# Encoder of a token tower: the products with the values one slot later, two dense units side by side, and the second norm between two pairs of row maxima

## The chip, the cores and the metric

One core of a Trainium2 chip runs the whole program. Its engines are TensorE (PE: matmuls; PEld: loading of their weights), VectorE (DVE), ScalarE (ACT), GpSimd (POOL) and SyncE (SP, which here only issues DMAs). The metric is the device time of one execution in microseconds; a kernel's time is the median of its runs.

## The reference

Eight sequences of 256 tokens, 256 features, float32 throughout. Four encoder layers come first. Then follow a second attention (16 heads of 64, windows of 128) and a mixture of 16 experts with two shared ones. The change touches the encoder alone:

```python
for l in range(4):
    y = layer_norm(h)                        # first norm
    q, k, v = y @ wq + bq, y @ wk + bk, y @ wv + bv      # 16 heads of 16
    p = softmax(q @ k.T / 4)                 # 256 x 256 a head
    h = h + (p @ v) @ wo + bo
    y = layer_norm(h)                        # second norm
    h = h + relu(y @ w1 + b1) @ w2 + b2      # 256 -> 1024 -> 256
```

## The kernel before, in words

**Jobs and slots.** The encoder is a pipeline of 32 jobs, one for each layer and sequence, `j` from 0 to 31. `for j in range(JOBS + 2)` with `for c in range(GROUPS)` inside gives every job four slots. In slot `(j, c)` TensorE computes the scores of four heads' pairs (`scores`, L401; four row strips of 32, so four matmuls go side by side into PSUM banks 0 to 3). VectorE takes their row maxima (`row_max`, L716), ScalarE takes the exponentials (`exps`, L547, two instructions for each of the four banks). In the next slot TensorE transposes the probabilities in four calls (`turn_probs` 0 to 3, L414) into banks 4 and 5 by turns. VectorE copies transpositions 0 and 2 out to `pts` (L724), ScalarE 1 and 3 (L556). So transposition 2 can start once copy 0 has freed bank 4, and transposition 3 once copy 1 has freed bank 5. Then come the products with the values (`pv`, L430; four column strips of 32, bank 6).

**Dense units.** Between these stand the wide matmuls of neighbouring jobs: in slot 0 the values of job j (L375) and half of the second feed-forward product of job j-2 (`ffn_down`, L458); in slot 1 the output projection of job j-1 (L375) and the other half; in slot 2 queries and keys of job j+1 (L367) and the first quarter of the first feed-forward product of job j-1 (`ffn_up`, L446); in slot 3 its other three quarters. A short transposition (L341) stands in each of slots 0 to 2: that of the softmax sums (`r_T`), of the first norm (`y_T`) and of the second norm (`y2_T`).

**What sets the order.** Each engine has one in-order instruction stream, which the code writes out by hand. The engines meet at semaphores, one pair for each PSUM bank (filled, freed). The list `order` says which bank each unit uses; a unit waits until the bank's last user has been taken out. VectorE also does the norms: `stats_of` writes mean and variance, GpSimd takes the root (L306), and `normalise` (L675, L677, L680) writes the normed rows. `attended` (L754) adds the output projection to `h`, `bias` (L747) the bias, `fed_forward` (L763) the second feed-forward product.

In this text a TensorE group is one call: eight matmul records for a dense unit (sixteen for half of `ffn_down`), eight for two transpositions of probabilities, four for a short one, sixteen for scores, thirty-two for products with the values.

Of the kernel before, what the change touches and what calls it, by code (L numbers as in the profile page):

```python
# [135 lines left out]
def embed_and_encoder(nc, io, h, ident, weights, wqkv, wout, norm, normab, gamma, pmk, w_yT, w_qT0, w_kT0):  # L136

    JOBS = L * B
    GROUPS = 4
    ctx = ExitStack()  # L140
    with ctx:
# [49 lines left out]
        def use(u, b):  # L191
            if 0 <= u[0] < JOBS:
                order.append((u, b))

        use((0, "yT"), 4), use((0, "q"), 7), use((0, "k"), 5)
        for j in range(JOBS + 2):
            for c in range(GROUPS):
                for n in range(4):
                    use((j, "S", 4 * c + n), n)
                if c == 0:  # L200
                    use((j, "v"), 7), use((j - 1, "rT"), 0), use((j - 2, "down", 0), 7)
                if c == 1:
                    use((j - 1, "wo"), 7), use((j + 1, "yT"), 0), use((j - 2, "down", 1), 7)
# [4 lines left out]
                jp, cp = divmod(GROUPS * j + c - 1, GROUPS)  # L208
                for n in range(4):
                    use((jp, "pt", 4 * cp + n), 4 + n % 2)  # L210
                if cp == 0:
                    use((jp, "o"), 6)
# [120 lines left out]
        def _(pe):  # L333
# [45 lines left out]
            def values(j):  # L379
                if j == 0:  # L380
                    pe.wait_ge(s_rest, 32)
                if real(j):
                    token_major(j, "v", yT[0], 2)

            def project_out(j):
                if real(j):
                    evacuated(pe, (j, "o"))
                    token_major(j, "wo", oT, 3)

            def scores(j, c):  # L390
                if not real(j):
                    return
                if c == 0:
                    evacuated(pe, (j, "q"))
                    evacuated(pe, (j, "k"))
                qt, ch = c // 2, c % 2
                gs = [acquire(pe, (j, "S", 4 * c + n)) for n in range(4)]
                for odd in range(2):
                    for n in range(4):
                        r = slice(32 * n, 32 * n + 32)  # L400
                        last = pe.matmul(gs[n][:, odd * S:(odd + 1) * S], qm[j % 2][r, odd, ch, qt * P:(qt + 1) * P],  # L401
                                         kT[j % 2][r, ch, :], start=True, stop=True)
                        if odd:
                            filled(last, (j, "S", 4 * c + n))
# [78 lines left out]
            feature_major(0, "k", 1)  # L483
            for j in range(JOBS + 2):
                for c in range(GROUPS):
                    jp, cp = divmod(GROUPS * j + c - 1, GROUPS)
                    scores(j, c)
                    if c == 0:
                        values(j)
                    if c == 1:  # L490
                        project_out(j - 1)
                    if c == 2:
                        feature_major(j + 1, "q", 0)
                    if c == 3:
                        ffn_up(j - 1, 1)
                    turn_probs(jp, cp, 0)
                    turn_probs(jp, cp, 1)
                    if c == 0:
                        r_T(j - 1)
                    if c == 1:  # L500
                        y_T(j + 1)
                    if c == 2:
                        y2_T(j - 1)
                    if c == 3:
                        ffn_up(j - 1, 2)
                    turn_probs(jp, cp, 2)
                    turn_probs(jp, cp, 3)
                    if (j, c) == (JOBS + 1, 0):
                        for u in SECOND[j, c]:
                            second(u)  # L510
                    if c < 2:
                        ffn_down(j - 2, c)
                    if c == 2:
                        feature_major(j + 1, "k", 1)
                    if c == 3:
                        ffn_up(j - 1, 3)
                    pv(jp, cp)
                    if (j, c) != (JOBS + 1, 0):
                        for u in SECOND.get((j, c), ()):
                            second(u)  # L520
                    if c == 2:
                        ffn_up(j - 1, 0)

        @block.scalar
        def _(act):
# [76 lines left out]
            for j in range(JOBS + 2):  # L602
                for c in range(GROUPS):
                    jp, cp = divmod(GROUPS * j + c - 1, GROUPS)
                    exps(j, c, 0)
                    exps(j, c, 1)
                    copy_pt(jp, cp, 1)
                    exps(j, c, 2)
                    if c == 0:
                        r_out(j - 1)  # L610
                    if c == 1:
                        y_out(j + 1, "yT", 0)
                    if c == 2:
# [5 lines left out]
                    if c != 2:  # L619
                        copy_pt(jp, cp, 3)  # L620
                    if c == 2:
                        k_out(j + 1)
                    for u in SECOND.get((j, c), ()):
                        second_out(u)
                    if c == 2:
                        relu(j - 1, 0)

        @block.vector
        def _(dve):
# [120 lines left out]
            def attended(j):  # L750
                if not real(j):
                    return
                g = take(dve, (j, "wo"))
                release(nc.vector.tensor_tensor(h[:, j % B], h[:, j % B], g[:].rearrange("p (i d) -> p i d", i=NT), ALU.add), (j, "wo"))  # L754
                evacuated(dve, (j, "wo"))
                bias(j, R_BO)

            def fed_forward(j, i):
                if not real(j):
# [33 lines left out]
            for j in range(JOBS + 2):  # L793
                for c in range(GROUPS):
                    jp, cp = divmod(GROUPS * j + c - 1, GROUPS)
                    if c == 0:
                        recips(j - 1)
                    if c == 1:
                        fed_forward(j - 2, 0)
                        o_norm(j - 1)  # L800
                    if c == 2:
                        fed_forward(j - 2, 1)
                    row_max(j, c, 0)
                    row_max(j, c, 1)
                    row_max(j, c, 2)
                    row_max(j, c, 3)
                    copy_pt(jp, cp, 0)
                    if c == 0:
                        v_out(j)
                        if j > 0:  # L810
                            stats_of(1, j + 1)
                    if c == 1:
# [6 lines left out]
                    copy_pt(jp, cp, 2)  # L819
                    if c == 0:  # L820
                        normalise(1, j + 1)
                    if c == 1:
                        normalise(2, j - 1)
                    if c == 2:
                        bias(j - 1, R_B2)
                    if c == 3:
                        relu(j - 1, 3)
                    if 0 <= GROUPS * (j - JOBS + 4) + c < 5:
                        second_norm(0, GROUPS * (j - JOBS + 4) + c)
                    if 0 <= GROUPS * (j - JOBS + 3) + c - 1 < 4:  # L830
                        second_norm(1, GROUPS * (j - JOBS + 3) + c - 1)
                    if (j, c) == (JOBS - 1, 0):
                        for w in range(NT):
                            nc.vector.tensor_copy(w_kT0[:, :, w, 0:PM], pmk[:, :, 0, :])
                    if (j, c) == (JOBS + 1, 0):
                        second_k_out(0)
                    if (j, c) == (JOBS + 1, 2):
                        for i in (1, 2, 3):
                            second_k_out(i)
# [1254 lines left out]
```

## Time and profile before

| | |
|---|---|
| median of 3 runs | 2105.56 us (2102.9 to 2107.07) |
| profiled execution | 2102.53 us, span 2100.7 us |
| TensorE clock granted, mean | 0.993 of full speed |
| busy over the span | PE 97%, PEld 79%, DVE 62%, ACT 49%, POOL 10% |
| encoder | first scores at 22.6 us, end of the stage at 1314 us |
| second attention, shared experts, experts | 1314 to 2101 us |

Matmuls are pipelined, so that a PE row is also busy while a matmul drains. What a group really costs is the time from its first start to the next group's first start, and that is how the rows below are to be read.

### The profile page before, as it was taken

What the parts mean: (1) busy time and instruction counts of PE and PEld (TensorE: products, weight loads), DVE (VectorE), ACT (ScalarE), POOL (GpSimd) and SP (SyncE); (2) the same over time, 40 slices, a digit from 0 to 9 for tenths busy, and PEclk for the clock granted to TensorE, in tenths of its full rate; (3) what the DMA queues carried; (4) which work ended last, traced back from release to release, by engine and by line L of the source; (5) the groups of instructions that cost most, each with busy time, mean ns of one, the idle gap of its engine ahead of it and who ended that gap; (6) DMA issues with size and microseconds to landing.
All of it is one profiled execution on the core that took longest, in us unless ns stands there. A gap on an engine that the chain in (4) does not pass through costs nothing. (4 is left out here: it accounts for less than half of the span.)

```text
span 2100.7 us, 42201 instructions
## 1 busy us (share of the span) xinstructions
PE 2037.0 (97%) x16462; PEld 1657.2 (79%) x16462; DVE 1299.0 (62%) x3344; ACT 1031.9 (49%) x3525; POOL 215.8 (10%) x251
## 2 busy tenths in 40 slices
PE   5899999999999999999999999899999999999998
PEld 4688888888888888888888877678788788877776
DVE  4676767676676776766767863767777646423322
ACT  3666656656566565666656552545445531111111
POOL 4000000000000000000000000000000000234444
PEclk9999999999999999999999999999999999999999
DMA  6000000100000400000000000500000100025542
GB/s 182 1 1 2 1 2 2 69 1 2 1 2 1 155 2 2 2 2 1 2 2 2 2 1 1 183 1 1 1 1 1 61 1 11 24 78 165 156 142 65
DMA packets 27203, 69.84 MB, mean 33 GB/s; under 512 B 9920, under 2 KB 17825, under 8 KB 23680
## 3 DMA queue, kind: packets, MB, share of 16 engines
q1 hardware_dynamic: 18432, 59.42, 8.4%
q0 software_dynamic: 6400, 5.63, 1.1%
q8 instruction: 134, 2.20, 0.4%
q10 hardware_dynamic: 2176, 2.10, 0.3%
q14 instruction: 61, 0.50, 0.1%
HBM read 61.16 MB, written 17.40 MB: 37 GB/s over the span
## 5 line engine op out<-in xcount | busy, mean ns | idle before, releaser
L547 ACT ACTIVATE probs<-bank,nmax 128x256 f32<-128x256 f32 x1024 | 474.4, 478 | 413.1 <-DVE nmax L716 413.1
L716 DVE TENSOR_REDUCE nmax<-bank 128x2 f32<-128x512 f32 x512 | 317.9, 683 | 208.6 <-PE bank L401 205.4
L414 PE MATMUL bank<-ident,probs 128*128 128x128 f32 x2048 | 271.9, 276 | 5.1 <-DVE pts L724 5.1
L414 PEld LDWEIGHTS bank<-ident,probs 128*128 128x128 f32 x2048 | 232.6, 141 | 39.7 <-DVE pts L724 22.5
L446 PE MATMUL bank<-yT,weights 128*128 128x256 f32 x1024 | 248.3, 386 | 0.9 <-ACT aT L570 0.9
L458 PE MATMUL bank<-weights,aT 128*128 128x256 f32 x1024 | 232.6, 380 | 1.3 <-DVE h L754 0.8
L547 ACT ACTIVATION_READ_ACCUMULATOR probs<-bank,nmax 128x1 f32 x1024 | 216.0, 211 | 0.0
L446 PEld LDWEIGHTS bank<-yT,weights 128*128 128x128 f32 x1024 | 184.5, 190 | 37.7 <-ACT aT L570 11.6
L458 PEld LDWEIGHTS bank<-weights,aT 128*128 128x128 f32 x1024 | 189.5, 190 | 25.3 <-DVE h L754 1.2
L724 DVE COPY pts<-bank 128x512 f32<-128x512 f32 x256 | 172.8, 675 | 38.6 <-PE bank L414 38.5
L556 ACT ACTIVATE pts<-bank 128x512 f32<-128x512 f32 x256 | 156.8, 612 | 21.4 <-PE bank L414 18.7
L306 POOL TENSOR_TENSOR sd<-mv,half 128x2 f32<-128x2 f32 x64 | 44.2, 690 | 1168.6 <-DVE mv L668 1168.6
L401 PE MATMUL bank<-kT,qm 32*128 32x256 f32 x2048 | 150.4, 408 | 3.7 <-ACT probs L547 2.8
L430 PE MATMUL bank<-pts,v 128*32 128x128 f32 x4096 | 140.9, 279 | 8.8 <-ACT pts L556 8.8
L430 PEld LDWEIGHTS bank<-pts,v 128*32 128x32 f32 x4096 | 105.9, 111 | 50.8 <-issue 38.9
L1334 ACT ACTIVATE w_probs<-w_bank,w_nmax 128x144 f32<-128x144 f32 x256 | 108.2, 536 | 75.6 <-DVE w_nmax L1499 75.6
L1890 PE MATMUL e_bank<-xeT,wqkv 128*128 128x320 f32 x512 | 140.8, 433 | 0.8 <-DVE xeT L1960 0.8
L367 PE MATMUL bank<-yT,weights 128*128 128x256 f32 x512 | 126.9, 392 | 1.2 <-ACT yT L534 1.2
L1890 PEld LDWEIGHTS e_bank<-xeT,wqkv 128*128 128x128 f32 x512 | 95.9, 190 | 39.0 <-issue 1.2
L1213 PE MATMUL w_bank<-xT_all,weights 128*128 128x256 f32 x512 | 121.1, 389 | 4.1 <-DVE weights L1594 2.9
L401 PEld LDWEIGHTS bank<-kT,qm 32*128 32x128 f32 x2048 | 94.6, 188 | 37.6 <-issue 28.4
L367 PEld LDWEIGHTS bank<-yT,weights 128*128 128x128 f32 x512 | 94.1, 194 | 23.2 <-issue 10.9
(218 smaller groups left out, 2935.4 us busy)
## 6 DMA issues: line engine op xcount, KB each, us to landing
wqkv<-in_experts SPq DMA_DIRECT2D x16, 1024.0 KB
weights<-in_wtok SPq DMA_DIRECT2D x4, 2048.0 KB, 19.0
wqkv<-in_experts SPq DMA_DIRECT2D x16, 512.0 KB
expert_rows<-xT_all SPq DMA_DIRECT2D x10, 546.0 KB, 16.5
xrows<-expert_rows SPq DMA_DIRECT2D x16, 273.0 KB
weights<-in_wtok SPq DMA_DIRECT2D x3, 1024.0 KB
wqkv<-in_wqkv SPq DMA_DIRECT2D x1, 3072.0 KB, 17.5
weights<-in_shared SPq DMA_DIRECT2D x1, 3072.0 KB, 10.8
```

What stands on the lines that cost most here:

```text
L367: last = pe.matmul(g[:, m * S:(m + 1) * S], wqkvo[buf(j)][:, n, k, m * P:(m + 1) * P], yT[0][:, k, :], start=(k == 0), stop=(k == KD - 1))
L401: last = pe.matmul(gs[n][:, odd * S:(odd + 1) * S], qm[j % 2][r, odd, ch, qt * P:(qt + 1) * P], kT[j % 2][r, ch, :], start=True, stop=True)
L414: last = pe.transpose(g[:, (NT * x + kb) * P:(NT * x + kb + 1) * P], p[:, x, kb * P:(kb + 1) * P], ident[:])
L430: last = pe.matmul(out, v[j % 2][:, kb, 4 * ch + n, x, :], pts[(4 * c + n) % 8][:, x, kb, :], start=(x == 0 and kb == 0), stop=(x == 1 and ...
L446: last = pe.matmul(g[:, m * S:(m + 1) * S], w1[buf(j)][:, k, f * P:(f + 1) * P], yT[1][:, k, :], start=(k == 0), stop=(k == KD - 1))
L458: last = pe.matmul(g[:, 0:D], aT[:, f, i * P:(i + 1) * P], w2[buf(j)][:, f, :], start=(f == 0), stop=(f == FT - 1))
L547: last = nc.scalar.activation(probs[u % 8][:, x, :], g[:, x * S:(x + 1) * S], ACT.Exp, bias=nmax[j % 2][:, col:col + 1], accum_out=rsum[j ...
L556: release(nc.scalar.activation(pts[(4 * c + n) % 8][:], g[:].rearrange("p (x k s) -> p x k s", x=2, k=NT), ACT.Copy), u)
L716: nc.vector.tensor_reduce(nmax[j % 2][:, col:col + 2], g[:].rearrange("p (x s) -> p x s", x=2), AX.X, ALU.max, negate=True).then_inc(s_max, 1)
L724: release(nc.vector.tensor_copy(pts[(4 * c + n) % 8][:], g[:].rearrange("p (x k s) -> p x k s", x=2, k=NT)), u)
L1213: last = pe.matmul(g[:, x * S:(x + 1) * S], w[e][:, k, m * P:(m + 1) * P], xT[:, k, (2 * t + a) * S:(2 * t + a + 1) * S], start=(k == 0), ...
L1890: last = pe.matmul(g[:, 0:CAP], (w1, w3)[x][a][:, k, m * P:(m + 1) * P], xeT[a][:, k, :], start=(k == 0), stop=(k == KD - 1))
```

## The change

The instructions and their sizes stay; the order on TensorE, ScalarE and VectorE and the use of the banks change.

- `pv` takes the group of two slots before, not of one, and stands right behind `scores`.
- Transpositions 0 and 1 follow it; then two dense units side by side (in slot 2 with `y2_T` between them); then transpositions 2 and 3, and at the slot's end `r_T`, `y_T` or the fourth unit.
- In slot 1 the second feed-forward product now precedes the output projection.
- The banks: in slot 0 `ffn_down` goes to bank 0 and `r_T` to 7, in slot 1 the projection to bank 1 and `y_T` to 7.
- ScalarE does all four `exps` of a slot in a row, then copy 1; the copies of `r_T` and `y_T` and the first `relu` move to the head of the following slot.
- VectorE: the second norm is written in slot 2 between row maxima 1 and 2; its statistics follow copy 2 of slot 1; `fed_forward` moves into the slot of its product; the bias of the projection is added a slot ahead of the projection.

```diff
@@ tensor
                     scores(j, c)
+                    pv(jq, cq)
+                    turn_probs(jp, cp, 0)
+                    turn_probs(jp, cp, 1)
                     if c == 0:
                         values(j)
+                        ffn_down(j - 2, 0)
                     if c == 1:
+                        ffn_down(j - 2, 1)
                         project_out(j - 1)
                     if c == 2:
                         feature_major(j + 1, "q", 0)
+                        y2_T(j - 1)
+                        feature_major(j + 1, "k", 1)
                     if c == 3:
                         ffn_up(j - 1, 1)
-                    turn_probs(jp, cp, 0)
-                    turn_probs(jp, cp, 1)
+                        ffn_up(j - 1, 2)
+                    turn_probs(jp, cp, 2)
+                    turn_probs(jp, cp, 3)
...
-                    pv(jp, cp)
...
@@ scalar
-                    exps(j, c, 0)
-                    exps(j, c, 1)
-                    copy_pt(jp, cp, 1)
-                    exps(j, c, 2)
...
+                    if c == 3:
+                        relu(j - 1, 0)
+                    for n in range(4):
+                        exps(j, c, n)
                     if c == 2:
                         y_out(j - 1, "y2T", 1)
-                        copy_pt(jp, cp, 3)
-                    exps(j, c, 3)
+                    copy_pt(jp, cp, 1)
+                    if c == 2:
+                        k_out(j + 1)
                     if c == 3:
                         relu(j - 1, 2)
...
+                    copy_pt(jp, cp, 3)
@@ vector
+                    row_max(j, c, 0)
+                    row_max(j, c, 1)
                     if c == 1:
-                        fed_forward(j - 2, 0)
                         o_norm(j - 1)
                     if c == 2:
-                        fed_forward(j - 2, 1)
+                        normalise(2, j - 1)
                     row_max(j, c, 2)
                     row_max(j, c, 3)
...
                     if c == 1:
+                        fed_forward(j - 2, 1)
                         attended(j - 1)
-                        stats_of(2, j - 1)
...
                     copy_pt(jp, cp, 2)
+                    if c == 1:
+                        stats_of(2, j - 1)
                     if c == 0:
                         normalise(1, j + 1)
-                    if c == 1:
-                        normalise(2, j - 1)
+                        bias(j - 1, R_BO)
```

How it stands on TensorE in slot 0 of a job in the steady pipeline, before. L401 are the scores, L375 the values, L414 transpositions of probabilities, L341 the short transposition, L458 half of the second feed-forward product, L430 the products with the values:

```order
L401 MATMUL bank<-kT,qm 128x256 x8
L375 MATMUL bank<-weights,yT 128x256 x4
L414 MATMUL bank<-ident,probs 128x128 x8
L341 MATMUL bank<-ident,rb 128x128 x4
L414 MATMUL bank<-ident,probs 128x128 x8
L458 MATMUL bank<-weights,aT 128x256 x8
L430 MATMUL bank<-pts,v 32x128 x16
```

And of the changed kernel, whose lines are numbered one higher here:

```order
L402 MATMUL bank<-kT,qm 128x256 x8
L431 MATMUL bank<-pts,v 32x128 x16
L415 MATMUL bank<-ident,probs 128x128 x8
L376 MATMUL bank<-weights,yT 128x256 x4
L459 MATMUL bank<-weights,aT 128x256 x8
L415 MATMUL bank<-ident,probs 128x128 x8
L342 MATMUL bank<-ident,rb 128x128 x4
```

The two column- and row-strip groups now stand side by side, and 12 dense matmuls stand between the two pairs of transpositions where 4 short ones stood.

TensorE in slot 2, before (L367 queries and keys, L446 the first quarter of the feed-forward product):

```order
L401 MATMUL bank<-kT,qm 128x256 x8
L367 MATMUL bank<-yT,weights 128x256 x4
L414 MATMUL bank<-ident,probs 128x128 x8
L341 MATMUL bank<-ident,yn 128x128 x4
L414 MATMUL bank<-ident,probs 128x128 x8
L367 MATMUL bank<-yT,weights 128x256 x4
L430 MATMUL bank<-pts,v 32x128 x16
L446 MATMUL bank<-yT,weights 128x256 x4
```

After:

```order
L402 MATMUL bank<-kT,qm 128x256 x8
L431 MATMUL bank<-pts,v 32x128 x16
L415 MATMUL bank<-ident,probs 128x128 x8
L368 MATMUL bank<-yT,weights 128x256 x4
L342 MATMUL bank<-ident,yn 128x128 x4
L368 MATMUL bank<-yT,weights 128x256 x4
L415 MATMUL bank<-ident,probs 128x128 x8
L447 MATMUL bank<-yT,weights 128x256 x4
```

The products no longer stand between two dense units.

VectorE from the projection of slot 1 to the end of the maxima of slot 2, before (L754 `attended`, L747 bias, L664 and L668 statistics, L724 copy 2, L675 to L680 the second norm, L763 `fed_forward`, L716 row maxima):

```order
L754 TENSOR_TENSOR h<-h,bank 128x512
L747 TENSOR_TENSOR h<-h,rows 128x512
L651 MEMSET scratch 128x1
L664 BN_STATS stats<-h 128x6 x2
L651 MEMSET scratch 128x1
L668 BN_AGGR mv<-stats 128x2 x2
L724 COPY pts<-bank 128x512
L675 TENSOR_SCALAR den<-sd 128x2
L677 RECIPROCAL rstd<-den 128x2
L680 TENSOR_SCALAR yn<-h,mv,rstd 128x256 x2
L763 TENSOR_TENSOR h<-h,bank 128x256
L716 TENSOR_REDUCE nmax<-bank 128x2 x4
```

After (the same work at L751, L720, L660, L664, L671 to L676, L712):

```order
L751 TENSOR_TENSOR h<-h,bank 128x512
L720 COPY pts<-bank 128x512
L647 MEMSET scratch 128x1
L660 BN_STATS stats<-h 128x6 x2
L647 MEMSET scratch 128x1
L664 BN_AGGR mv<-stats 128x2 x2
L712 TENSOR_REDUCE nmax<-bank 128x2 x2
L671 TENSOR_SCALAR den<-sd 128x2
L673 RECIPROCAL rstd<-den 128x2
L676 TENSOR_SCALAR yn<-h,mv,rstd 128x256 x2
L712 TENSOR_REDUCE nmax<-bank 128x2 x2
```

The second norm has moved out of slot 1 and stands between the second and the third row maximum of slot 2.

## Rows read from the trace of the kernel before

**Rows 1.** Busy time by stretch (start:end, length, engines, clock), slots of the filling pipeline.
```profile
41.18:50.64 9.46, 9.11 (x85) 7.06 (x81) 5.58 (x10) 5.72 (x20) 0.54 (x1) 0.85 0.00 1
50.64:58.93 8.29, 4.82 (x69) 3.66 (x65) 4.55 (x8) 4.73 (x18) 0.00 (x0) 0.93 0.01 2
58.93:68.91 9.98, 7.85 (x80) 6.05 (x77) 6.50 (x20) 5.32 (x19) 0.72 (x1) 0.84 0.00 0
68.91:79.72 10.81, 8.25 (x79) 6.45 (x76) 7.78 (x19) 5.75 (x20) 0.68 (x1) 0.82 0.01 2
79.72:90.64 10.92, 10.92 (x96) 8.55 (x93) 6.08 (x11) 6.47 (x22) 0.00 (x0) 0.91 0.01 2
90.64:99.85 9.21, 9.21 (x89) 7.66 (x88) 5.46 (x11) 6.40 (x22) 0.00 (x0) 1.00 0.01 2
```

**Rows 2.** Timeline of TensorE, slot 3: start, duration, line, out<-in, records.
```profile
405.39 1.89 PE L446 MATMUL bank<-yT,weights 128*128 128x256 f32 x8
407.12 1.04 PE L414 MATMUL bank<-ident,probs 128*128 128x128 f32 x8
```

**Rows 3.** Timeline of TensorE, slot 0.
```profile
410.82 1.15 PE L401 MATMUL bank<-kT,qm 32*128 32x256 f32 x16
411.90 1.99 PE L375 MATMUL bank<-weights,yT 128*128 128x256 f32 x8
413.73 1.04 PE L414 MATMUL bank<-ident,probs 128*128 128x128 f32 x8
414.61 0.60 PE L341 MATMUL bank<-ident,rb 128*128 128x128 f32 x4
415.12 1.09 PE L414 MATMUL bank<-ident,probs 128*128 128x128 f32 x8
416.05 3.64 PE L458 MATMUL bank<-weights,aT 128*128 128x256 f32 x16
419.63 1.08 PE L430 MATMUL bank<-pts,v 128*32 128x128 f32 x32
420.64 0.71 PE L401 MATMUL bank<-kT,qm 32*128 32x256 f32 x8
```

**Rows 4.** Timeline of TensorE, slot 2, its head and its end.
```profile
430.43 1.15 PE L401 MATMUL bank<-kT,qm 32*128 32x256 f32 x16
...
437.55 1.08 PE L430 MATMUL bank<-pts,v 128*32 128x128 f32 x32
...
440.48 1.15 PE L401 MATMUL bank<-kT,qm 32*128 32x256 f32 x16
```

**Rows 5.** Timeline of VectorE, slots 1 and 2.
```profile
421.80 2.48 DVE L716 TENSOR_REDUCE nmax<-bank 128x2 f32<-128x512 f32 x4 [0.23 <-PE bank L401]
424.20 0.68 DVE L724 COPY pts<-bank 128x512 f32<-128x512 f32 x1
...
426.24 0.42 DVE L664 BATCH_NORM_STATS2 stats<-h 128x6 f32<-128x256 f32 x1
...
428.08 0.17 DVE L675 TENSOR_SCALAR den<-sd 128x2 f32<-128x2 f32 x1 [0.23 <-POOL sd L306]
...
428.48 0.74 DVE L680 TENSOR_SCALAR yn<-h,mv,rstd 128x256 f32<-128x256 f32 x2
```

**Rows 6.** Timeline of ScalarE, slot 2.
```profile
432.38 0.47 ACT L547 ACTIVATE probs<-bank,nmax 128x256 f32<-128x256 f32 x1 [3.95 <-DVE nmax L716]
...
435.35 0.48 ACT L547 ACTIVATE probs<-bank,nmax 128x256 f32<-128x256 f32 x1
...
435.80 1.03 ACT L534 ACTIVATE yT<-bank,cols 128x256 f32<-128x256 f32 x2
436.70 0.62 ACT L556 ACTIVATE pts<-bank 128x512 f32<-128x512 f32 x1
```

**Rows 7.** Timeline of ScalarE and TensorE in the filling pipeline.
```profile
56.58 0.65 ACT L556 ACTIVATE pts<-bank 128x512 f32<-128x512 f32 x1
...
57.37 1.63 PE L430 MATMUL bank<-pts,v 128*32 128x128 f32 x32 [1.37 <-ACT pts L556]
```

More of the change, by code:

```diff
@@ L199, in embed_and_encoder @@
                     use((j, "S", 4 * c + n), n)
+                jp, cp = divmod(GROUPS * j + c - 1, GROUPS)
+                jq, cq = divmod(GROUPS * j + c - 2, GROUPS)
+                if cq == 0:
+                    use((jq, "o"), 6)
+                for n in range(4):
+                    use((jp, "pt", 4 * cp + n), 4 + n % 2)
                 if c == 0:
-                    use((j, "v"), 7), use((j - 1, "rT"), 0), use((j - 2, "down", 0), 7)
+                    use((j, "v"), 7), use((j - 2, "down", 0), 0), use((j - 1, "rT"), 7)
                 if c == 1:
-                    use((j - 1, "wo"), 7), use((j + 1, "yT"), 0), use((j - 2, "down", 1), 7)
+                    use((j - 2, "down", 1), 7), use((j - 1, "wo"), 1), use((j + 1, "yT"), 7)
                 if c == 2:
@@ L207, in embed_and_encoder @@
                     use((j - 1, "up", 1), 7), use((j - 1, "up", 2), 0), use((j - 1, "up", 3), 7)
[L208 to L212, printed above, removed]
                 for n, u in enumerate(SECOND.get((j, c), ())):
@@ L486, in _ @@
                     jp, cp = divmod(GROUPS * j + c - 1, GROUPS)
+                    jq, cq = divmod(GROUPS * j + c - 2, GROUPS)
                     scores(j, c)
+                    pv(jq, cq)
+                    turn_probs(jp, cp, 0)
+                    turn_probs(jp, cp, 1)
+                    if (j, c) == (JOBS + 1, 0):
+                        for u in SECOND[j, c]:
+                            second(u)
                     if c == 0:
                         values(j)
+                        ffn_down(j - 2, 0)
                     if c == 1:
+                        ffn_down(j - 2, 1)
                         project_out(j - 1)
@@ L501, in _ @@
                         y_T(j + 1)
[L502 to L516, printed above, removed]
-                    pv(jp, cp)
                     if (j, c) != (JOBS + 1, 0):
@@ L522, in _ @@
                         ffn_up(j - 1, 0)
+                    if c == 3:
+                        ffn_up(j - 1, 3)
         @block.scalar
@@ L604, in _ @@
                     jp, cp = divmod(GROUPS * j + c - 1, GROUPS)
-                    exps(j, c, 0)
-                    exps(j, c, 1)
-                    copy_pt(jp, cp, 1)
-                    exps(j, c, 2)
-                    if c == 0:
+                    if c == 1:
                         r_out(j - 1)
-                    if c == 1:
+                    if c == 2:
                         y_out(j + 1, "yT", 0)
+                    if c == 3:
+                        relu(j - 1, 0)
+                    for n in range(4):
+                        exps(j, c, n)
                     if c == 2:
                         y_out(j - 1, "y2T", 1)
-                        copy_pt(jp, cp, 3)
-                    exps(j, c, 3)
+                    copy_pt(jp, cp, 1)
+                    if c == 2:
+                        k_out(j + 1)
                     if c == 3:
                         relu(j - 1, 2)
[L619 to L622, printed above, removed]
+                    copy_pt(jp, cp, 3)
                     for u in SECOND.get((j, c), ()):
                         second_out(u)
-                    if c == 2:
-                        relu(j - 1, 0)
         @block.vector
@@ L752, in attended @@
                     return
+                step.wait(dve)
                 g = take(dve, (j, "wo"))
@@ L755, in attended @@
                 evacuated(dve, (j, "wo"))
-                bias(j, R_BO)
             def fed_forward(j, i):
@@ L811, in _ @@
                             stats_of(1, j + 1)
+                        fed_forward(j - 2, 0)
                     if c == 1:
+                        fed_forward(j - 2, 1)
                         attended(j - 1)
[L814 removed]
                     if c == 2:
@@ L819, in _ @@
                     copy_pt(jp, cp, 2)
+                    if c == 1:
+                        stats_of(2, j - 1)
                     if c == 0:
                         normalise(1, j + 1)
-                    if c == 1:
-                        normalise(2, j - 1)
+                        bias(j - 1, R_BO)
                     if c == 2:
+                        if real(j - 1):
+                            dve.wait_ge(s_yn[1], j)
                         bias(j - 1, R_B2)
```

2 lines of the change are left out of this document (removed).

## The prediction, written before the changed kernel ran

> **What bounds the kernel now.** I read the summary of the busy times first, then the busy time by stretch, then the timeline of TensorE alone over one job, and last the timelines of VectorE and ScalarE beside it. The summary puts TensorE at 97% of the span. In a slot of the steady pipeline it is busy for the whole of it, 9.21 of 9.21 us, at the full clock of 2.4 GHz, with VectorE at 5.46 and ScalarE at 6.40 [rows 1]. So TensorE sets the encoder's pace, and the question is what its slots hold besides work. The Trainium skill says of that (Trainium Kernel Development and Optimization, Performance Expectations) that matmul busy time is a bad measure since matmuls are pipelined; this trace agrees, the row of 9.21 busy us hides all that follows.
>
> Distances from start to start show it. I call the matmuls of 128 rows and columns full, the scores (32 rows) and the products with the values (32 columns) strips.
> - A full dense unit of eight records takes 1.73 between full ones (405.39 to 407.12) [rows 2], and 1.83 behind scores (411.90 to 413.73) [rows 3]. Between products and scores it takes 1.92 (2.93 from 437.55 to 440.48, less 1.01 for the products) [rows 4]; less the 0.10 that it pays behind strips that is 1.82 before scores alone.
> - Two transpositions take 0.88 (413.73 to 414.61), and 0.93 where their first had to wait or follows strips (415.12 to 416.05) [rows 3]. So one takes 0.44.
> - Scores take 1.08 to what follows (410.82 to 411.90); products 1.01 before scores (419.63 to 420.64) [rows 3].
> - The short transposition takes 0.51 (414.61 to 415.12), 0.44 for its four records and 0.07 of waiting for VectorE's copy 0, which frees bank 4 [rows 3].
>
> Every change between strips and full, or between the two strips, thus costs about 0.2, half at the end of the one, half at the head of the other; waits for data are small. The lengths are: slot 0 9.82 (410.82 to 420.64), slot 1 9.79 (to 430.43) [rows 3, 4], slot 2 10.05 (430.43 to 440.48) [rows 4], slot 3 9.21 [rows 1]. A job takes 38.87.
>
> **The change part by part.**
>
> *Order on TensorE.* I add the new order up from the same distances.
> - Slot 0: scores 1.08, products 1.01, transpositions behind strips 0.93, values 1.73, second feed-forward product 2 x 1.73 = 3.46, transpositions 0.88, short one with the change to scores 0.44 + 0.09 = 0.53: 9.62. That is 0.20 less.
> - Slot 1 has the same parts: 9.62, 0.17 less.
> - Slot 2: 1.08 + 1.01 + 0.93 + 1.73 + 0.44 + 1.73 + 0.88 + 1.82 = 9.62, 0.43 less. One pair of changes is gone here, as the products no longer stand between two dense units.
> - Slot 3: 1.08 + 1.01 + 0.93 + 3.46 + 0.88 + 1.82 = 9.18, 0.03 less.
>
> Without new waits a job takes 38.04, which is 0.83 less.
>
> *Products right behind scores.* The trace has no such pair. Products took 1.01 behind full units, and scores 1.08 before them [rows 3]. Low end: these two less the 0.1 that either change costs at its border, should two strip groups overlap. High end: products pay at their head what a dense unit pays behind scores, 0.10 [rows 3, 2]. I take 1.08 and 1.01, because each is the group's own row, and keep 0.10 a slot, 0.4 a job, for the range.
>
> *Waits that go.* Transposition 2 now stands behind 5.2 us of dense work in slots 0 and 1 and behind 3.9 in slot 2, so copy 0 is long done. The products wait for copies 2 and 3 of the slot before; ScalarE's copy 3 ends 0.3 to 0.4 after the scores start, and VectorE's copy 2 in slot 1 ends about 0.2 after it, and the products start at 1.08. That cover is 0.7.
>
> *Waits that come: slot 2.* Times from the scores' first start.
> 1. VectorE. In slot 1 the projection is now the last dense unit; its last record ends at 1.08 + 1.01 + 0.93 + 3.46 + 1.73 and some 0.15 of drain = 8.36. Then come the addition and copy 2 (0.68 for a copy as wide [rows 5], and the same for the addition) and the statistics (about 1.05 of the 1.84 from 426.24 to 428.08; the rest is GpSimd's root) [rows 5]. VectorE is free at 10.85, which is 1.24 of slot 2.
> 2. Row maxima take 0.62 each (2.48 for four) [rows 5]: 0 and 1 end at 2.48. The root was ready at 2.0. The second norm takes 1.14 (428.08 to 429.22) [rows 5]: 3.64.
> 3. Exponentials start 0.72 behind their maximum (1.95 from the scores' start to the first, of which 1.23 to the first maximum) [rows 4, 6] and follow each other at 0.45 (435.35 to 435.80) [rows 6]. Those of banks 2 and 3 run from 4.37 to 6.18.
> 4. ScalarE then writes out the second norm's transposition, 0.90 to its next start (435.80 to 436.70), and only then copy 1, 0.62 [rows 6]: 7.70. TensorE starts 0.14 behind the end of such a copy (57.23 to 57.37) [rows 7]: 7.84.
> 5. TensorE has queued transposition 3 behind 1.08 + 1.01 + 0.93 + 1.73 + 0.44 + 1.73 + 0.44 = 7.36. It waits 0.48 and restarts at 0.05: 0.53. Behind it wait the first feed-forward quarter and the next scores.
>
> So slot 2 takes 10.15, 0.1 more than before. The bounds are 0 (if ScalarE gets to copy 1 half a us sooner) and 1.0 (if the norm's root comes late by as much as its 0.5 of slack). In slots 0, 1 and 3 copy 1 ends at about 6.9, 6.9 and 6.3, and transposition 3 stands at 8.6, 8.6 and 6.9; the least cover is 0.6.
>
> *Banks.* Bank 0 for the feed-forward product in slot 0 is asked for at 4.75, and its exponentials are out at 3.4. Its addition on VectorE ends at 8.8, and the next scores want the bank at 9.6. Bank 7 for that quarter in slot 2 needs the queries' copy, which ends at 7.5, before 7.8. I cost them at nothing; the last is the thinnest.
>
> *VectorE.* Its work of a job is unchanged. In slot 0 the first norm and the bias now reach 1.8 us into slot 1, which puts that slot's exponentials 0.6 later, covered as above.
>
> Steady sum: -0.83 + 0.53 = -0.30 a job, over the 30 jobs in which the pipeline is full: -9.
>
> **The filling of the pipeline.** Five slots from 41.18 to 90.64 take 9.46, 8.29, 9.98, 10.81 and 10.92 with the clock at 0.82 to 0.93 [rows 1]: TensorE waits for the last copies before the products (1.37 in one place [rows 7]), and after such waits runs part of the way at 1.2 GHz. Products a slot later take that wait away. What is late next is the chain scores, exponentials, copy 1, transposition 3: 1.95 + 8 x 0.45 + 0.62 + 0.14 + 0.44 = 6.8, with the short transposition 7.3. By that the five slots are 7.4 (sum of TensorE's parts), 6.8, 7.3, 8.6 (1.3 for a VectorE that starts late by its norm and bias) and 10.15: 40.2 for 49.5, or -9. Some time at 1.2 GHz will stay, as waits of 1.4 us remain. I take -8, bounds -4 and -10.5. The drain of the pipeline has the same units in another order; I leave it at nothing, within 1.5.
>
> **Sum.** -9 - 8 = -17 on the profiled 2102.5 (span 2100.7 and 1.8 around it) gives 2085.5. The median of the runs shown is 3.0 above the profiled execution, so 2088.6 there; I say 2088.
>
> **The rivals.**
> - *The wait of slot 2 doesn't come* (or is under 0.15), because ScalarE is ahead of my chain. For it: ScalarE is busy 6.4 of 9.2 [rows 1]. Against it: the chain is in order and each link has a row. Then 30 x 0.83 = 25 and 8: 2105.6 - 33 = 2073. Chance 0.16.
> - *Other waits take the gain*: copies or bank 7 late in a slot where I see 0.3 to 0.7 of cover; the job gives back its 0.3, and only some of the filling stays. 2098 to 2109. For it: VectorE runs later than before in three slots of four. Against it: no cover is under 0.3. Chance 0.12.
> - *Scores and products side by side cost more than apart*, which ends slower. Place: the four new pairs in each job. If the products can't start until the last scores have left the array and their own weights are then loaded, each pair pays up to 0.3 more, 30 x 4 x 0.3 = 36, so 2088 + 36 = 2124; the change is slower from 17 / 120 = 0.14 a pair. Against it: products followed by scores, the same pair turned round, cost 1.01 and no more [rows 3]. Chance 0.08. The Trainium skill (TensorEngine Tiling (Array Packing), Key Properties) says that a change of tiling mode drains TensorE. It gives no price; by it the four pairs each pay a whole change, and so they do in my sum, at the rows' 0.2; the trace agrees for the turned pair, and no run so far shows this one.
> - That the change doesn't do what it says is excluded by the order shown ahead.
>
> **How the numbers follow.** The forecast has 0.64 and its own range is 2077 to 2097. The rivals have 0.16 below, 0.12 around no change and 0.08 above. The range reaches down to 2072 and up to 2101. About 0.2%, some 4 us, is what a measurement of this kernel can tell from no change. Faster by more: 0.64 + 0.16 + 0.04 = 0.84; within it 0.07; slower 0.09.
>
> **What would show it.** In the timeline of TensorE after: scores to products 1.08, products to transpositions 1.01, transpositions 0.93; slots 0 and 1 at 9.6, slot 3 at 9.2 and a wait of about 0.5 at transposition 3 of slot 2, put down to ScalarE's copy. Before 91 us, slots of 7 to 9 us and a clock above 0.9. I am wrong if slots 0, 1 or 3 show a wait over 0.1, if scores to products takes over 1.2, or if slot 2 is under 9.8.

## The result and the profile after

The changed kernel takes 2074.07 us (median of 4 runs, 2070.51 to 2075.57) against 2105.61 for the kernel before: ratio 0.9851, 95% interval [0.9836, 0.9867]. The profiled execution has a span of 2072.9 us against 2100.7. The forecast was 2088, with a range of its own of 2077 to 2097; the measured time lies 3 us below that range.

The sum was -17, the measured change of the span is -27.8 (the medians differ by 31.5, the change timed once more below by 27.2). Cut at the first starts of the score groups in both traces, it falls apart as follows (us):

| stretch | before | after | difference |
|---|---|---|---|
| start to the first scores | 22.56 | 22.07 | -0.5 |
| filling, jobs 0 and 1 | 77.30 | 69.11 | -8.2 |
| jobs 2 to 27 | 1010.67 | 993.38 | -17.3 |
| jobs 28 to 30 | 118.18 | 116.97 | -1.2 |
| job 31 to the end of the encoder | 84.97 | 86.15 | +1.2 |
| second stage to its first transposition | 12.97 | 11.06 | -1.9 |
| the rest | 774.1 | 774.2 | +0.1 |

Two rows of this table can't be put to the change. In the second stage's row the granted clock was 0.87 in the trace before and 1.00 in the one after. Over all twelve traces of this document that stretch takes 11.0 to 11.6 us where the clock is 1.00, and 12.4 to 14.5 where it is lower, whatever the order. The rest takes 774.0 to 774.3 in five of the twelve and 776.0 to 776.1 in seven; that this pair agrees to 0.1 says little.

TensorE alone, slot 0 of a job in the steady pipeline (start, duration, group), to be read against [rows 3]:

```profile
396.83 1.15 PE L402 MATMUL bank<-kT,qm 32*128 32x256 f32 x16
397.91 1.08 PE L431 MATMUL bank<-pts,v 128*32 128x128 f32 x32
398.92 1.09 PE L415 MATMUL bank<-ident,probs 128*128 128x128 f32 x8
399.85 1.89 PE L376 MATMUL bank<-weights,yT 128*128 128x256 f32 x8
401.58 3.62 PE L459 MATMUL bank<-weights,aT 128*128 128x256 f32 x16
405.03 1.04 PE L415 MATMUL bank<-ident,probs 128*128 128x128 f32 x8
405.91 0.60 PE L342 MATMUL bank<-ident,rb 128*128 128x128 f32 x4
406.44 0.93 PE L402 MATMUL bank<-kT,qm 32*128 32x256 f32 x12
```

From start to start the distances are 1.08, 1.01, 0.93, 1.73, 3.45, 0.88 and 0.53: the slot is 9.61 long, with no wait in it. Scores followed by products, the pair that the trace of before did not show, cost what they cost apart.

Slot 2, the same view, against [rows 4]:

```profile
416.04 1.15 PE L402 MATMUL bank<-kT,qm 32*128 32x256 f32 x16
...
422.95 1.26 PE L415 MATMUL bank<-ident,probs 128*128 128x128 f32 x8
424.05 1.89 PE L447 MATMUL bank<-yT,weights 128*128 128x256 f32 x8
425.87 0.70 PE L402 MATMUL bank<-kT,qm 32*128 32x256 f32 x6
```

Transpositions 2 and 3 take 1.10 and not 0.88: here is the new wait, 0.22 with its restart, and the slot is 9.83 long. VectorE and ScalarE show what it hangs on; VectorE first:

```profile
417.16 0.15 DVE L664 BATCH_NORM_AGGREGATE mv<-stats 128x2 f32<-128x6 f32 x1
417.23 1.26 DVE L712 TENSOR_REDUCE nmax<-bank 128x2 f32<-128x512 f32 x2
418.41 0.16 DVE L671 TENSOR_SCALAR den<-sd 128x2 f32<-128x2 f32 x1
...
418.80 0.74 DVE L676 TENSOR_SCALAR yn<-h,mv,rstd 128x256 f32<-128x256 f32 x2
...
419.46 1.28 DVE L712 TENSOR_REDUCE nmax<-bank 128x2 f32<-128x512 f32 x2
```

ScalarE in the same slot:

```profile
420.17 0.47 ACT L547 ACTIVATE probs<-bank,nmax 128x256 f32<-128x256 f32 x1 [0.31 <-DVE nmax L712]
...
421.99 1.03 ACT L534 ACTIVATE yT<-bank,cols 128x256 f32<-128x256 f32 x2
422.88 0.62 ACT L556 ACTIVATE pts<-bank 128x512 f32<-128x512 f32 x1
```

The chain is the forecast one: the statistics keep VectorE until the maxima start at 1.19 of the slot, the norm stands between the two pairs, and ScalarE writes out `yT` before copy 1, which ends at 7.46. The links on VectorE are shorter than I took them, and so is the step from copy 1 to TensorE; those on ScalarE have the forecast lengths.

Slots of the filling pipeline, busy time by stretch, against [rows 1]. They are slot 3 of job 0 and slots 0 to 2 of job 1; the last figures of a row are the granted clock, the share of the DMA engines and GB/s:

```profile
46.85:53.59 6.74, 4.42 (x64) 3.25 (x65) 4.73 (x9) 4.77 (x18) 0.00 (x0) 1.00 0.00 0
53.59:61.68 8.09, 8.04 (x77) 6.12 (x76) 4.62 (x12) 5.22 (x19) 0.00 (x0) 0.79 0.01 2
61.68:72.18 10.50, 8.07 (x77) 6.32 (x76) 7.21 (x18) 5.28 (x20) 0.72 (x1) 0.84 0.01 2
72.18:82.01 9.83, 9.83 (x93) 8.04 (x93) 8.28 (x22) 7.77 (x25) 0.69 (x1) 1.00 0.01 2
```

The first three are 6.74, 8.09 and 10.50 for 8.29, 9.98 and 10.81. In the middle two the clock is at 1.2 GHz for part of the way (0.79 and 0.84 of full speed): behind a wait of 2.43 us the projection takes 3.44 (67.29 to 70.73) where it takes 1.73 at full clock. In a second profile of the same kernel these two slots took 7.21 and 8.12.

### The profile page after: what moved, and what is told of

It is laid out like the page before. It is cut to its first block and busy times, and to the rows that moved or that the text cites. A ratio compares the mean times of both kernels' runs of the same rounds, so it can differ in the third digit from the quotient of the medians.

```text
span 2072.9 us, 42265 instructions
## 1 busy us (share of the span) xinstructions
PE 2013.2 (97%) x16462; PEld 1659.8 (80%) x16462; DVE 1299.1 (63%) x3344; ACT 1039.5 (50%) x3525; POOL 215.8 (10%) x251
## 5 line engine op out<-in xcount | busy, mean ns | idle before, releaser
L547 ACT ACTIVATE probs<-bank,nmax 128x256 f32<-128x256 f32 x1024 | 469.4, 481 | 230.3 <-DVE nmax L712 230.3
L712 DVE TENSOR_REDUCE nmax<-bank 128x2 f32<-128x512 f32 x512 | 322.1, 681 | 78.0 <-PE bank L402 78.0
L415 PE MATMUL bank<-ident,probs 128*128 128x128 f32 x2048 | 281.6, 278 | 12.6 <-DVE pts L720 6.9
L447 PE MATMUL bank<-yT,weights 128*128 128x256 f32 x1024 | 237.9, 381 | 0.9 <-ACT aT L570 0.9
L720 DVE COPY pts<-bank 128x512 f32<-128x512 f32 x256 | 175.6, 686 | 59.0 <-PE bank L415 55.3
L447 PEld LDWEIGHTS bank<-yT,weights 128*128 128x128 f32 x1024 | 188.1, 191 | 23.2 <-ACT aT L570 1.3
L368 PE MATMUL bank<-yT,weights 128*128 128x256 f32 x512 | 123.0, 385 | 1.2 <-ACT yT L534 1.2
L1212 PEld LDWEIGHTS w_bank<-xT_all,weights 128*128 128x128 f32 x512 | 95.3, 192 | 17.9 <-DVE weights L1593 3.6
```

What stands on the lines that cost most here:

```text
L368: last = pe.matmul(g[:, m * S:(m + 1) * S], wqkvo[buf(j)][:, n, k, m * P:(m + 1) * P], yT[0][:, k, :], start=(k == 0), stop=(k == KD - 1))
L415: last = pe.transpose(g[:, (NT * x + kb) * P:(NT * x + kb + 1) * P], p[:, x, kb * P:(kb + 1) * P], ident[:])
L447: last = pe.matmul(g[:, m * S:(m + 1) * S], w1[buf(j)][:, k, f * P:(f + 1) * P], yT[1][:, k, :], start=(k == 0), stop=(k == KD - 1))
L547: last = nc.scalar.activation(probs[u % 8][:, x, :], g[:, x * S:(x + 1) * S], ACT.Exp, bias=nmax[j % 2][:, col:col + 1], accum_out=rsum[j ...
L712: nc.vector.tensor_reduce(nmax[j % 2][:, col:col + 2], g[:].rearrange("p (x s) -> p x s", x=2), AX.X, ALU.max, negate=True).then_inc(s_max, 1)
L720: release(nc.vector.tensor_copy(pts[(4 * c + n) % 8][:], g[:].rearrange("p (x k s) -> p x k s", x=2, k=NT)), u)
```

## Experiments

Eight edits in ten runs, one of them the changed kernel again and one a repetition. In what follows "a job" is one of the steady ones, from score group to score group: 38.87 before, 38.20 after (slots 9.60, 9.60, 9.83, 9.17).

### The changed kernel again

> The changed kernel itself, beside the three that build on it, so that they are compared on one chip: 2074 us, 0.985 of the kernel before. Its trace, like the first, should show slots of 9.60, 9.60, 9.83 and 9.17 us.

Measured: 2077.22 us, ratio 0.9871 [0.9856, 0.9886]; slots 9.60, 9.60, 9.83, 9.17. It is the base for the three that were timed beside it. Its filling takes 67.9 us, 1.2 less than in the first trace, and it has the low clock (0.86) at the second stage's start.

### The wait of slot 2 is the output that stands before copy 1

```diff
-                    if c == 2:
-                        y_out(j - 1, "y2T", 1)
                     copy_pt(jp, cp, 1)
                     if c == 2:
+                        y_out(j - 1, "y2T", 1)
                         k_out(j + 1)
```

> ScalarE takes copy 1 ahead of the output of the second norm's transposition in slot 2. Theory: the 0.22 us that transposition 3 waits in slot 2 is that output (0.90 from start to start) standing before copy 1; now copy 1 ends at 6.6 of the slot and transposition 3 stands at 7.4, so slot 2 falls from 9.83 to 9.61, 30 times 0.22 = 6.6 us, and up to 1 us more in slot 2 of the last job: 2067 us. Rival: the wait only moves to the first feed-forward quarter, which stands right behind and needs that output as well as the queries' copy: slot 2 stays within 0.1 of 9.83, 2074 us.

Measured: 2069.74 us, ratio 0.984 [0.9822, 0.9858], 7.5 under the changed kernel beside it; repeated, 2066.88 us, 0.983 [0.9809, 0.985]. Slot 2 of the timeline of TensorE:

```profile
413.40 1.15 PE L402 MATMUL bank<-kT,qm 32*128 32x256 f32 x16
...
420.31 1.04 PE L415 MATMUL bank<-ident,probs 128*128 128x128 f32 x8
421.18 1.89 PE L447 MATMUL bank<-yT,weights 128*128 128x256 f32 x8
423.01 0.50 PE L402 MATMUL bank<-kT,qm 32*128 32x256 f32 x4
```

The pair of transpositions is back at 0.87, the slot at 9.61, a job at 37.98. So the wait was that one link, and with it gone no wait is left in the steady job. Slot 2 of job 31 gains as well, 9.75 for 11.82 in the changed kernel beside it, where I had expected at most 1; the granted clock in that slot was 1.00 here and 0.86 there. The rival, that it moves on to the first feed-forward quarter, falls: that stands 0.87 behind the pair, without a wait. This version beats both kernels.

### The place of the second norm

Undone alone: `normalise(2, j - 1)` stands behind `stats_of(2, j - 1)` in slot 1 again.

```diff
-                    if c == 2:
-                        normalise(2, j - 1)
...
                     if c == 1:
                         stats_of(2, j - 1)
+                        normalise(2, j - 1)
```

> One part undone: the second norm stands at the end of slot 1 again, behind its statistics, all else as in the changed kernel. Theory: the place between two pairs of maxima is what keeps the dense order alive. Here VectorE waits for GpSimd's root until 1.95 of slot 2 and starts the row maxima at 3.05 and not 1.19; the exponentials end at 7.4, copy 1 at 8.9, and transposition 3, which stands at 7.4, waits 1.6: slot 2 takes 11.3, +1.5 a job, 30 x 1.5 = +44: 2118 us. Rival: its place is neutral because VectorE is busy 71% only: 2074 us.

Measured: 2123.59 us, ratio 1.011 [1.0086, 1.0133], slower than the kernel before. Slot 2 takes 11.36, a job 39.74. VectorE waits for the root where the maxima could run, and they start at 3.13 of the slot (430.71 is its start):

```profile
432.78 0.17 DVE L671 TENSOR_SCALAR den<-sd 128x2 f32<-128x2 f32 x1 [0.80 <-POOL sd L307]
...
433.84 2.48 DVE L712 TENSOR_REDUCE nmax<-bank 128x2 f32<-128x512 f32 x4
```

The other end of the chain, on TensorE:

```profile
438.37 0.60 PE L415 MATMUL bank<-ident,probs 128*128 128x128 f32 x4
439.76 0.66 PE L415 MATMUL bank<-ident,probs 128*128 128x128 f32 x4 [0.79 <-ACT pts L556]
```

Copy 1 on ScalarE, which it waits for:

```profile
439.06 0.65 ACT L556 ACTIVATE pts<-bank 128x512 f32<-128x512 f32 x1
```

A third thing came beside the forecast: a wait of 0.25 at the keys, for bank 1's exponentials. That the dense order pays at all hangs on the norm's new place, which is worth 1.53 a job here.

### Dense units side by side, but the products where they were

```diff
-                    pv(jq, cq)
                     turn_probs(jp, cp, 0)
...
                     if c == 3:
                         ffn_up(j - 1, 3)
+                    pv(jp, cp)
```

The list of banks follows the order.

> One part undone: products with the group of the slot before, at the slot's end behind transpositions 2 and 3 (and what follows them); the dense units stay side by side. Theory: the later products are needed for the rest. Here the products wait for ScalarE's copy 3 in slots 0 and 1 (0.5 each), and everything behind the scores comes 1 us sooner, so that transposition 3 waits for copy 1 by 1.1 in slot 2 and 0.4 in slot 3, and the change of form costs 0.05 more a slot: +2.5 a job: 2145 us. Rival: the gain is that of the dense units side by side alone, and the products' place is worth only its form changes: 2080 us.

Measured: 2153.88 us, ratio 1.0258 [1.0236, 1.028]. A job takes 40.53, +2.33 for a forecast of +2.5; the slots are 10.01, 10.17, 10.84 and 9.51. The profiled execution was the fastest of the four, 2146.20; the median is 9 above the forecast of 2145. Slot 0's products wait for ScalarE's copy 3, right behind the short transposition:

```profile
428.22 0.60 PE L342 MATMUL bank<-ident,rb 128*128 128x128 f32 x4
429.16 1.08 PE L431 MATMUL bank<-pts,v 128*32 128x128 f32 x32 [0.34 <-ACT pts L556]
```

and transposition 3 of slot 2 for copy 1:

```profile
447.86 0.66 PE L415 MATMUL bank<-ident,probs 128*128 128x128 f32 x4 [1.01 <-ACT pts L556]
```

### The later products alone, on the kernel before

```diff
                     scores(j, c)
+                    pv(jq, cq)
...
-                    pv(jp, cp)
```

> One part alone on the kernel before: products of two slots before, right behind the scores; the rest in its old order. Theory: slot 2 saves one pair of form changes (0.18), but the output projection in slot 1, which stands right behind, waits for VectorE's product with the reciprocal sums (about 1.05), so +0.9 a job, +26 in all, while the filling of the pipeline saves about 5: 2127 us. Rival: the later products bring the whole gain by themselves: 2085 us or less.

Measured: 2117.66 us, ratio 1.0088 [1.0063, 1.0112]. The forecast was 2127. A job takes 39.56, +0.69 for a forecast of +0.9, with slots of 9.80, 10.76, 9.78 and 9.22; the filling takes 72.1 us, 5.2 less than before. The wait stands where it was expected, at the projection of slot 1:

```profile
423.07 1.08 PE L430 MATMUL bank<-pts,v 128*32 128x128 f32 x32
425.06 1.99 PE L375 MATMUL bank<-weights,oT 128*128 128x256 f32 x8 [0.91 <-DVE oT L741]
```

Slots 0 and 3 stay within 0.02 of the kernel before, in which the products already stood right in front of the next scores there; slot 2 alone falls, from 10.05 to 9.78, as one pair of changes is spared there (forecast 0.18). The 0.20 of slots 0 and 1 in the changed kernel thus comes with the rest of the order, not with the products' place alone.

This run and the one above are the two halves of the change. Either is slower than the kernel before, and only both together are faster.

### The price of a change of form

```diff
                     scores(j, c)
-                    pv(jq, cq)
                     turn_probs(jp, cp, 0)
                     turn_probs(jp, cp, 1)
+                    pv(jq, cq)
```

> The changed kernel with the products behind transpositions 0 and 1, not before them: one more pair of form changes a slot, with no unit moved by more than 1 us and all waits covered as before. It prices the change of form by itself. Theory: from the distances of starts a pair costs 0.20 (0.06 and 0.12 into and out of full before the products, 0.21 out of them into a dense unit, less 0.19 for scores and products side by side), 0.79 a job: +24 us, 2098 us. Rival: scores and products side by side hide nothing, the order within the slot is free: 2074 us.

Measured: 2090.65 us, ratio 0.9958 [0.9944, 0.9972], 7 below the forecast of 2098. Slots 0, 1 and 3 take 9.80, 9.80 and 9.36, which is 0.20 more each, as forecast. Slot 2 stays at 9.84, which the forecast had missed: its extra 0.20 goes into the wait for copy 1. A job takes 38.79, 0.59 more and not 0.79. Slot 0:

```profile
397.61 1.15 PE L402 MATMUL bank<-kT,qm 32*128 32x256 f32 x16
398.68 1.09 PE L415 MATMUL bank<-ident,probs 128*128 128x128 f32 x8
399.71 1.08 PE L431 MATMUL bank<-pts,v 128*32 128x128 f32 x32
400.72 1.99 PE L376 MATMUL bank<-weights,yT 128*128 128x256 f32 x8
402.55 3.62 PE L459 MATMUL bank<-weights,aT 128*128 128x256 f32 x16
```

The transpositions take 1.03 for 0.93 and the values 1.83 for 1.73. The order within a slot is not free, and no wait shows it. The rival of a free order is out.

### Products of two groups in every second slot

On top of the copy first.

```diff
-                    pv(jq, cq)
+                    if c % 2:
+                        pv(*divmod(GROUPS * j + c - 3, GROUPS))
+                        pv(jq, cq)
```

> On top of the copy first: products of two groups side by side in slots 1 and 3, none in slots 0 and 2, which spares two of the eight changes into and out of the products' form in a job. Theory: a spared pair is worth 0.14 us (0.02 at the products' head, 0.11 at their end), 0.27 a job, 8 us in all, but transposition 3 of slot 2 then stands at 6.35 with copy 1 out at 6.6, and the first feed-forward quarter at 6.8 with the queries' copy out at 7.1, which gives back about 0.3: within 4 us of the kernel with the copy first, about 2067 us. Rival: form changes cost nothing and only the waits count: slots 0 and 2 wait for what came 1 us sooner, and the time is 2075 us or more.

Measured: 2086.31 us, ratio 0.992 [0.9907, 0.9934], 17 above the kernel with the copy first: a miss. The rival's number (2075 or more) came true, but not its reason. The spared changes are there: slots 0 and 1 together take 8.59 + 10.48 = 19.07 for 19.20, 0.13 less. But slot 2 takes 9.44 where 8.60 would be its work:

```profile
423.30 1.37 PE L415 MATMUL bank<-ident,probs 128*128 128x128 f32 x8
424.93 1.99 PE L447 MATMUL bank<-yT,weights 128*128 128x256 f32 x8 [0.25 <-ACT yT L536]
```

From the transpositions to the quarter 1.63 pass and not 0.88. The row of 1.37 (1.04 with the copy first) holds the wait for copy 1, and then the quarter waits 0.25 for the norm's output, which the copy ahead of it had put off. I had counted the queries' copy for that place and not this. Without the products in slot 2, TensorE comes too early for both.

### The final norm's steps

The changed kernel loses 1.0 and 0.9 in slots 2 of jobs 28 and 29 (10.87 and 10.78), where VectorE also does steps of the final norm. The kernel before loses in these jobs too, 0.8 each in slots 0 of jobs 29 and 30. On top of the copy first, two other placings:

```diff
-                    if 0 <= GROUPS * (j - JOBS + 4) + c < 5:
-                        second_norm(0, GROUPS * (j - JOBS + 4) + c)
...
+                    for s, n in {(JOBS - 4, 0): [(0, 0)], (JOBS - 4, 2): [(0, 1)],
+                                 (JOBS - 4, 3): [(0, 2), (0, 3)],
...
```

> On top of the copy first: the eight steps of the final norm that VectorE does in jobs 28 to 30 are kept out of slot 1. Theory: VectorE has no slack from the end of slot 1 to the row maxima of slot 2, and the steps that stand there lengthened slot 2 of jobs 28 and 29 from 9.83 to 10.87 and 10.78: 2 us go, of which about 1 comes back in slot 0 behind two steps at once: 1 us under the kernel with the copy first, 2066 us. Rival: these two slots are long for another reason, and stay at 10.8.

Measured: 2070.7 us, ratio 0.9845 [0.9831, 0.9858], no change from the kernel with the copy first, where 1 us less was forecast. Its slot 2 of job 28 and slots 0 of jobs 29 and 30:

```profile
1096.80:1106.41 9.61, 9.61 (x93) 8.06 (x92) 8.98 (x26) 7.67 (x25) 0.69 (x1) 1.00 0.01 2
1115.58:1126.82 11.24, 9.84 (x93) 8.13 (x92) 9.99 (x32) 4.57 (x18) 1.38 (x2) 1.00 0.01 1
1155.20:1166.21 11.01, 9.84 (x94) 8.13 (x93) 9.74 (x28) 4.58 (x18) 0.69 (x1) 1.00 0.01 1
```

The long slots are cured, which is 1.7 us, and 2.7 come back where two steps stand ahead of slot 0 at once (9.80 and 9.77 with the copy first): the forecast had 1 for that. The other placing puts one step at a time into slots 2 and 3 of jobs 26 to 31, and moves their roots on GpSimd along:

```diff
...
+                    if (j, c) in STEPS:
+                        second_norm(*STEPS[j, c])
                     if c == 3:
                         relu(j - 1, 3)
...
```

> The kernel with the copy first, and the final norm's steps on VectorE spread over jobs 26 to 31, one at a time, only into slots 2 and 3, in slot 3 ahead of the last relu, where VectorE is idle for 1.4 to 2 us. Theory: these steps cost time only because they stood where VectorE has no slack (slot 1 into 2, and two at once into slot 0). Slots 2 of jobs 28 and 29 fall from 10.48 and 10.40 to 9.61, slots 0 of jobs 29 and 30 from 9.80 and 9.77 to 9.60: 2.0 us under the kernel with the copy first. Rival: the steps cost VectorE time wherever they stand, and another slot grows by what these lose, as it did when they were moved two at a time.

> The kernel with the copy first once more, as the base for the spread steps on the same chip: 0.984 of the kernel before, about 2070 us, slots of 9.60, 9.60, 9.61 and 9.17 us.

Measured: 2068.24 us, ratio 0.9829 [0.9816, 0.9842], beside 2066.88 for the repetition: the same within the intervals. Jobs 28 to 30 take 113.94, just 3 x 37.98, and 2.0 less than with the copy first, as forecast. But two other stretches are longer in this trace, slot 2 of job 31 and the second stage up to its first transposition:

```profile
1211.06:1222.29 11.23, 8.53 (x77) 6.19 (x77) 8.09 (x26) 6.33 (x21) 1.38 (x2) 0.85 0.00 1
1277.91:1292.43 14.52, 11.39 (x33) 5.14 (x33) 7.38 (x28) 4.89 (x19) 3.49 (x7) 0.76 0.87 294
```

The same two in the repetition of the copy first:

```profile
1212.38:1222.12 9.74, 7.04 (x77) 5.10 (x77) 6.76 (x18) 6.33 (x21) 0.69 (x1) 1.00 0.01 3
1277.73:1288.83 11.10, 8.44 (x32) 4.08 (x33) 7.39 (x28) 4.75 (x19) 3.50 (x7) 1.00 0.94 306
```

The difference is the granted clock, but for 0.5 us in the second stage, where a wait for the first probabilities lasts 3.13 and not 2.65. The step of the final norm that now stands in slot 2 of job 31 is not it: up to the feed-forward quarter the two timelines of TensorE agree to 0.01, and then the quarter alone takes 3.41 for 1.93:

```profile
1218.88 3.48 PE L447 MATMUL bank<-yT,weights 128*128 128x256 f32 x8 [0.25 <-ACT yT L534]
```

```profile
1220.19 1.99 PE L447 MATMUL bank<-yT,weights 128*128 128x256 f32 x8 [0.26 <-ACT yT L534]
```

The first is of the spread steps, with a clock of 0.55 from 1218.88 to 1222.29, the second of the repetition. The run before this one has the same quarter at 3.34 and a clock of 0.57, with no step in that slot. Why the clock falls in some traces and not in others stays open. The theory on where VectorE has room holds for the jobs; the 2 us that it gave there are too few to show in the time of the kernel.

## Why the prediction was right, and where its size was off

- **What bounds.** TensorE's own order, not its waits. Held: jobs 2 to 27 carry the main part, 17.3 of 27.8, where TensorE is busy for all but 0.2 us in both traces.
- **The distances.** Slots 0, 1 and 3 were forecast at 9.62, 9.62 and 9.18 and measured at 9.60, 9.60 and 9.17. The distances of the kernel before carry over to another order, scores beside products included (1.08). The rival of the dear pair is out; its 0.3 a pair came from no row, and the measured excess is nothing. The run with the products behind the transpositions prices one more pair of changes at 0.20.
- **The wait of slot 2: the mis-sized term.** Forecast 0.53, measured 0.22; 30 x 0.31 = 9 us of the 11 between forecast and span. I had named a slot under 9.8 as a sign of being wrong, and 9.83 is barely above it. The place, the releaser and the order of the links were right, as the run with the copy first shows. The sizes: I had set the norm at 2.48 and the third maximum at 3.64, measured 2.37 (418.41) and 3.42 (419.46); the exponentials at 4.37, measured 4.13; copy 1's end at 7.70, measured 7.46 (423.50). I had added durations where VectorE's instructions overlap: the norm's first starts at 418.41 while the maxima before it end at 418.49, and the third maximum at 419.46 while the norm ends at 419.54. The start of the chain was also added up wrongly: the parts named for VectorE make 10.77 and not 10.85, which is 1.15 of slot 2; measured 1.19. The last 0.1 is the step from ScalarE's copy to TensorE. I took 0.14 from a row of the filling [rows 7]; here the pair's 1.10 leaves about 0.05, and in the run with the norm back copy 1 ends at 439.71 and TensorE starts at 439.76. The rival that saw no wait here put it at under 0.15; 0.22 is nearer to that than to 0.53, and its 2073 was nearer than my 2088. Its reason, a ScalarE ahead of my chain, was not the cause: ScalarE's own links had the forecast lengths, VectorE's were shorter.
- **The filling.** Forecast -8, measured -8.2, in part by luck. The five slots that I had summed fell by 5.9 only (49.5 to 43.5): slot 2 of job 0 took 8.38 for a forecast of 7.4, and slots 0 and 1 of job 1 took 8.09 and 10.50 for 7.3 and 8.6, all three at 1.2 GHz for part of the way (clock 0.90, 0.79 and 0.84). The other 2.2 came from the first two slots, which my sum left out; the longer of them, 12.78 before and 10.65 after, takes 8.1 to 12.4 in the other ten traces. In the second profile of the changed kernel the five fell by 8.7, the whole filling by 9.4. The later products alone took 5.2 off it; the rest belongs to the rest of the order or to the clock, which no run separates.
- **The end.** I left it at nothing within 1.5. It is +1.2 in job 31, and nothing behind it. In slot 2 of that job TensorE waits for transpositions 2 and 3, the feed-forward quarter then takes 2.91 (1229.15 to 1232.06) at a clock of 0.62, and the slot takes 11.63 for 9.76; the other slots give back 0.7. I had not looked at jobs 28 and 29 either, where the final norm's steps fall just where the new order has no room. Their slots 2 lose 2.0 us and slots 0 of jobs 29 and 30 0.4, but the kernel before lost 1.6 in those slots 0, so that only 0.8 of it counts in the change. The second stage reached its first transposition 1.9 sooner at its higher granted clock; in its second profile the same kernel has the low clock there and takes 12.4, so I put this to no part of the change.
- **That the halves hang together** stood in no sentence of the prediction. The later products make room for the dense units side by side, and the norm's place pays for them; the later products alone are slower than the kernel before, and so is the changed kernel with either the products or the norm put back. The norm's place alone, and the dense units undone alone, were not run.

## What to carry to other kernels

When TensorE is busy throughout, write down the distance from start to start of every group, sorted by what stands before it. Those distances add up to the time of another order within 0.02 us a slot here, changes of tile form included, as long as no wait comes in. For the chain on the engines that feed it do the same, and don't add durations. Then look for the one engine that is late at the head of a slot, and ask which of the things it does there the next matmul waits for: turning two of ScalarE's instructions round was worth another 0.3 to 0.4%.

## What I had not expected of the hardware

A change between groups of full matmuls and of strips costs TensorE about 0.1 us at either border (0.05 at the head of transpositions) while it shows as busy. One more pair of changes cost 0.20, the same in three slots of every job (9.80 for 9.60). The end of a strip group costs the same before the other strips as before full matmuls: scores take 1.08 before products and before values, products 1.01 before scores and before transpositions. Where the slot had a wait of 0.22 anyway, the extra 0.20 did not show at all (9.84 for 9.83).
